# Cross attention in a decoder block: softmax denominators from TensorE, inverse by logarithm on ScalarE, biases added in halves, and an earlier passage from the recurrence

## The reference

```
x = x + slot_attention(layernorm(x))                 # gated recurrence over tokens, 4 heads, 64 slots
q, k, v = layernorm(x) @ Wq.T + bq, ctx @ Wk.T + bk, ctx @ Wv.T + bv      # 16 heads of 8
scores = q k^T * 8**-0.5 + attn_mask; -inf where padded; + fside + fside  # fside: (32, 16, 128, 128), 33.5 MB
x = x + softmax(scores) v @ Wo.T + bo
x = x + experts(layernorm(x))                        # gated low-rank experts around a 128-512-128 network
```

## Time and profile before

| | us |
|---|---|
| three runs | 633.39, 636.18, 636.24 (median 636.18) |
| the profiled execution | 633.74 |
| its span | 632.0 |
| recurrence, roughly | 0 to 225 |
| cross attention, roughly | 225 to 480 |
| experts, roughly | 480 to 632 |

### The profile page before, as it was taken

How to read it: one execution, slowest core, us unless ns; L and a number is a source line. 1 busy time by engine, 2 the same in 40 slices (tenths; PEclk the granted TensorE clock), 3 DMA queues, 4 the chain that set the end, 5 groups by cost and what they waited for, 6 DMA issues and landing times. The chain is left out here.

```text
span 632.0 us, 15993 instructions
## 1 busy us (share of the span) xinstructions
PE 512.1 (81%) x4272; PEld 378.5 (60%) x4272; DVE 499.0 (79%) x2009; ACT 428.9 (68%) x1545; POOL 369.5 (58%) x392
## 2 busy tenths in 40 slices
PE   4788988989987567877777777777766899999986
PEld 3566766766765435555555555555545678888864
DVE  2677777777776359999999999999986588888872
ACT  3667777777774239999999999999984133333321
POOL 6245364364454667888888888888842144444430
PEclk9899999999998869999999999999997599999999
DMA  6900000000000076888888888888700000000000
GB/s 172 229 10 1 1 2 0 0 0 0 2 0 2 9 130 114 153 143 146 147 146 146 144 142 141 141 141 146 133 2 2 0 18 19 17 17 17 19 18 17
DMA packets 84423, 42.37 MB, mean 67 GB/s; under 512 B 4379, under 2 KB 84133, under 8 KB 84389
## 3 DMA queue, kind: packets, MB, share of 16 engines
q1 hardware_dynamic: 83234, 41.63, 35.8%
q10 hardware_dynamic: 1154, 0.33, 0.2%
HBM read 39.86 MB, written 2.10 MB: 66 GB/s over the span
## 5 line engine op out<-in xcount | busy, mean ns | idle before, releaser
L944 ACT ACTIVATE c_P<-c_P,c_min 128x128 f32<-128x128 f32 x512 | 204.7, 461 | 0.0
L1113 POOL TENSOR_TENSOR c_bias<-c_fside,c_cm 128x2048 f32<-128x2048 f32 x32 | 145.5, 4547 | 2.3 <-DVE c_cm L1030 2.3
L944 ACT ACTIVATION_READ_ACCUMULATOR c_P<-c_P,c_min 128x1 f32 x512 | 132.5, 260 | 0.0
L1005 DVE CUSTOM_DVE_ANT_0 c_P<-banks,c_bias 128x128 f32<-128x128 f32 x512 | 117.2, 287 | 8.0 <-issue 3.7
L900 PE MATMUL banks<-ident,c_P 128*128 128x128 f32 x512 | 80.9, 285 | 8.3 <-ACT c_P L944 6.7
L900 PEld LDWEIGHTS banks<-ident,c_P 128*128 128x128 f32 x512 | 57.5, 144 | 23.2 <-ACT c_P L944 13.4
L1040 DVE COPY shared<-banks 128x512 f32<-128x512 f32 x96 | 66.1, 688 | 2.8 <-PE banks L900 2.8
L1455 POOL TENSOR_TENSOR xs<-shared,xs 128x512 fp32r<-128x512 f32 x8 | 10.8, 1345 | 88.5 <-ACT xs L1287 88.5
L1220 PE MATMUL banks<-um,lb_s 128*128 128x512 f32 x192 | 57.7, 417 | 2.7 <-ACT shared L1277 1.9
L748 POOL TENSOR_TENSOR lower<-meanvar,minus_one 128x2 f32<-128x2 f32 x16 | 3.4, 211 | 79.9 <-DVE meanvar L639 79.7
L1277 ACT ACTIVATE shared<-banks,bi_col 128x512 f32<-128x512 f32 x32 | 22.0, 688 | 41.2 <-PE banks L1220 41.2
(11 more groups left out here) (197 smaller groups left out, 1375.4 us busy)
## 6 DMA issues: line engine op xcount, KB each, us to landing
c_fside<-in_fside_Bx16xSxS_dram SPq DMA_DIRECT2D x64, 512.0 KB, 7.1
c_ctx<-in_ctx_dram SPq DMA_DIRECT2D x32, 64.0 KB, 5.2
out_dram<-shared SPq DMA_DIRECT2D x8, 256.0 KB, 2.3
X<-in_x_dram SPq DMA_DIRECT2D x3, 512.0 KB, 5.1
kmask_sb<-in_mask_BxS_bf_dram SPq DMA_DIRECT2D x1, 512.0 KB, 7.4
X<-in_x_dram SPq DMA_DIRECT2D x2, 128.0 KB, 3.4
c_P<-in_L_ffn_wi_dram SPq DMA_DIRECT2D x1, 256.0 KB
c_P<-in_L_ffn_lora_B_dram SPq DMA_DIRECT2D x1, 256.0 KB
```

The costliest lines, as they stand in the source:

```text
L944: last = nc.scalar.activation(P[:, par, h, :], P[:, par, h, :], ACT.Exp, bias=mn[:, par, h:h + 1], scale=-1.0, accum_out=rsx[:, par, h:h + 1])
L1005: last = nc.vector.tensor_tensor_reduce(out=P[:, o, h, :], in0=bank(SCORE_BANKS[i])[:, 128 * j:128 * j + 128], in1=fm[:, o, h, :], scale=- ...
L1113: nc.gpsimd.tensor_tensor(fm[:, q, :, :], fs[:, q, :, :], bc(cm[:], XH), ALU.add).then_inc(C["fm"], 1)
```

## The change

- `exps` no longer writes row sums. Instead `mix_values` runs a second set of 16 products (32 instructions) with blocks of ones in the place of the values, so bank 7, columns 128 to 255, holds each head's sum, already turned and spread over its 8 rows. ScalarE takes the logarithm of that block and the exponential of its negative. Reciprocals, spreading, their transpose and copy go.
- ScalarE copies turned tokens and context in one instruction, and takes over the values copy from VectorE. Its order in a step is exponentials 1, inputs, exponentials 2 and 3, logarithm, inverse, keys, queries, exponentials 0 of the next batch, values, turned weights 3.
- TensorE's order is scores, inputs, weights 0, mix, queries and keys, weights 1, values, weights 2 and 3, output projection. The values product is a semaphore step of its own, apart from the output projection.
- VectorE's order is mask, statistics, score 0, weights 0, aggregate, scores 1 and 2, outputs, weights 1, score 3, normalise, add to the stream, weights 2. The mask block has two buffers.
- Biases are added, waited for and loaded in two halves of 8 heads, and in step n for batch n+1, no longer for n+2. GpSimd's order is first half, output bias, second half, roots, keys spread; its steps before 0 have no biases. Those of batch 0 are added in recurrence steps 4 and 5, of batch 1 in 14 and 15.
- The passage: step -3 comes after recurrence step 15 on GpSimd and VectorE; steps -2, -1, 0, 1 on all engines after recurrence steps 16, 17, 18, 19. The scores of the first two batches use banks 0, 1, 5, 4, with waits on TensorE for what the recurrence still holds.

The diff, cut to its core:

```diff
+            pool_step(pool, nc.gpsimd.memset(head_ones[:].rearrange("p (j w) -> p j w", j=XG)[:, :, 0:XD], 1.0))
...
+        def x_masks(dve, k, q):
+            need(dve, C["fm"], 2 * k - 2)
...
+        def x_biases(pool, k, m, q, half):
+            heads = slice(HALF * half, HALF * half + HALF)
+            need(pool, C["cm"], k + 1)
+            need(pool, s_fs[q][half], 16 * (m + 1))
+            need(pool, C["tt"], 4 * k - 6 + 2 * half)
+            nc.gpsimd.tensor_tensor(fm[:, q, heads, :], fs[:, q, heads, :], bc(cm[:, q, :], HALF), ALU.add).then_inc(C["fm"], 1)
...
+            def values():
                 if project:
+                    need(pe, C["q"], n + 3)
...
+                nc.tensor.matmul(bank(0)[:, 128:256], xcT[:, o, 1, :], x_wT[:, 2, :], start=True, stop=True).then_inc(C["vp"], 1)
...
                 need(pe, C["v"], n)
+                need(pe, C["oT"], n - 1)
+                for w in range(2):
+                    for j in range(XG):
+                        for i in range(NI):
+                            block = vp[:, o, VPAD * i + 32 * j:VPAD * i + 32 * j + 32] if w == 0 else head_ones[:, 32 * j:32 * j + 32]
+                            last = nc.tensor.matmul(bank(7)[32 * i:32 * i + 32, 128 * w:128 * w + 128], block,
+                                                    PTs[:, o, i, 128 * j:128 * j + 128], start=(j == 0), stop=(j == XG - 1))
                 last.then_inc(C["pv"], 1)
+            def project_out():
+                need(pe, C["oT"], n)
+                need(pe, C["x2"], n - 1)
+                need(pe, C["v"], n + 2 if scores else min(n + 1, B))
...
-                    last = nc.scalar.activation(P[:, par, h, :], P[:, par, h, :], ACT.Exp, bias=mn[:, par, h:h + 1], scale=-1.0,
-                                                accum_out=rsx[:, par, h:h + 1])
+                    last = nc.scalar.activation(P[:, par, h, :], P[:, par, h, :], ACT.Exp, bias=mn[:, par, h:h + 1], scale=-1.0)
...
-                nc.scalar.copy(xT2[:], bank(0)[:, 0:128])
-                nc.scalar.copy(cT[:, q, :], bank(0)[:, 128:256]).then_inc(C["T"], 1)
+                nc.scalar.copy(xcT[:, q, :, :].rearrange("p w t -> p (w t)"), bank(0)[:, 0:256]).then_inc(C["T"], 1)
...
+            def denominator_logs():
+                need(act, C["pv"], n)
+                need(act, C["rc"], n - 1)
+                nc.scalar.activation(log_den[:], bank(7)[:, 128:256], ACT.Ln).then_inc(C["ln"], 1)
+            def denominators_inverted():
+                need(act, C["ln"], n)
                 need(act, C["oT"], n - 1)
+                nc.scalar.activation(inv_den[:], log_den[:], ACT.Exp, scale=-1.0).then_inc(C["rc"], 1)
...
-                need(dve, C["fm"], n + 2)
+                need(dve, C["fm"], 2 * n + 3 + i // 2)
...
+            if isinstance(n, int) and n < 0:
+                if norm:
+                    roots()
+                if project:
+                    keys_apart()
+                    output_bias()
+                return
+            biases = scores and not (isinstance(n, int) and n < 1)
+            if biases:
+                x_biases(pool, n + 1, m + q, o, 0)
             if project:
                 output_bias()
-                biases()
-                keys_apart()
+            if biases:
+                x_biases(pool, n + 1, m + q, o, 1)
             if norm:
                 roots()
+            if project:
+                keys_apart()
...
-                need(sp, C["fm"], n - 1)
...
-                    rows = slice(64 * half, 64 * half + 64)
-                    sp.dma_start(fs[rows, q, :, :], bias[rows, :, :]).then_inc(s_fs[q], 16)
+                    heads = slice(HALF * half, HALF * half + HALF)
+                    need(sp, C["fm"], 2 * n - 3 + half)
+                    sp.dma_start(fs[:, q, heads, :], bias[:, heads, :]).then_inc(s_fs[q][half], 16)
...
+            for t in range(4, 6):
+                gsa_peeled(gsa, t)
+                x_biases(pool, 0, 0, 0, t - 4)
             gsa_loop(pool, gsa)
+            for t in range(PAIRS - 2, PAIRS):
                 gsa_peeled(gsa, t)
+                x_biases(pool, 1, 0, 1, t - PAIRS + 2)
             pool.wait_ge(G["xn"], PAIRS)
             x_peeled(cross, -3)
+            gsa_peeled(gsa, PAIRS)
...
+            for k in range(4):
+                x_peeled(cross, k - 2)
+                if k < 3:
+                    gsa_peeled(gsa, PAIRS + 1 + k)
             x_loop(pool, cross)
...
+            pe.wait_ge(G["rt"], PAIRS - 1)
+            pe.wait_ge(G["x1"], PAIRS - 1)
+            x_peeled(cross, 0)
+            pe.wait_ge(C["ptD"], 3)
+            pe.wait_ge(C["ptA"], 1)
+            gsa_peeled(gsa, PAIRS + 3)
             pe.wait_ge(G["un"], PAIRS)
+            pe.wait_ge(G["rt"], PAIRS)
             pe.wait_ge(G["x1"], PAIRS)
+            x_peeled(cross, 1)
             x_loop(pe, cross)
```

More of the change, by code:

```diff
@@ L133, in decoder @@
         lb_s = sb("lb_s", [128, 2, F], fp32r)
-        SHARED = 20736
+        SHARED = 18432
         shared = sb("shared", [128, SHARED])
@@ L949, in inputs_turned, with keys, queries @@
                 need(act, C["Tp"], n + 3)
-                need(act, C["yv"], n + 1)
-                nc.scalar.copy(xT2[:], bank(0)[:, 0:128])
-                nc.scalar.copy(cT[:, q, :], bank(0)[:, 128:256]).then_inc(C["T"], 1)
-            def queries_keys():
+                need(act, C["vp"], n + 1)
+                nc.scalar.copy(xcT[:, q, :, :].rearrange("p w t -> p (w t)"), bank(0)[:, 0:256]).then_inc(C["T"], 1)
+            def keys():
+                need(act, C["qkp"], n + 3)
+                need(act, C["kbd"], n + 2)
+                nc.scalar.activation(kx[:], bank(0)[:, 128:256], ACT.Identity, bias=bk_col[:]).then_inc(C["k"], 1)
+            def queries():
                 need(act, C["qkp"], n + 3)
@@ L975, in x_scalar @@
                 inputs_turned()
-            if finish:
-                reciprocals_turned()
             if attend:
                 exps(n, q, 2)
+                exps(n, q, 3)
+            if finish:
+                denominator_logs()
+                denominators_inverted()
             if project:
-                queries_keys()
-            if attend:
-                exps(n, q, 3)
+                keys()
+                queries()
             if scores:
                 exps(n + 1, o, 0)
+                values()
             if attend:
@@ L1070, in x_vector @@
                 weights_turned(0)
+            if norm:
+                aggregates()
             if scores:
                 score(1)
+                score(2)
+            if finish:
+                outputs()
             if attend:
@@ L1075, in x_vector @@
             if scores:
-                score(2)
-            if finish:
-                outputs()
-            if scores:
                 score(3)
-            if attend:
-                weights_turned(2)
-            if scores:
-                values()
+            if norm:
+                normalise()
             if finish:
@@ L1568, in _ @@
             act.wait_ge(s_xw, XW)
[L1569 to L1576 removed]
+            act.wait_ge(G["s"], PAIRS)
+            act.wait_ge(G["silu"], PAIRS)
+            for k in range(4):
+                x_peeled(cross, k - 2)
+                if k < 3:
+                    gsa_peeled(gsa, PAIRS + 1 + k)
             x_loop(act, cross)
@@ L1611, in _ @@
             gsa_peeled(gsa, 3)
+            dve.wait_ge(s_km, 16)
+            for k in range(2):
+                x_masks(dve, k, k)
             dve.wait_ge(s_x[4], 16)
@@ L1616, in _ @@
             gsa_loop(dve, gsa)
-            for t in range(PAIRS - 2, PAIRS + 1):
+            for t in range(PAIRS - 2, PAIRS):
                 gsa_peeled(gsa, t)
```

171 lines of the change are left out of this document (60 added, 111 removed).

## The result

The changed kernel takes 682.35 us (median of 4 runs, 681.54 to 682.77); the kernel before took 634.78 beside it (4 runs, 631.74 to 636.24). The ratio is 1.0754, with an interval of [1.0707, 1.0802]: 7.5% slower, where 609 us had been forecast. The profiled execution has a span of 681.1 us.

What follows compares the result with a forecast made beforehand. The prediction took ScalarE to bound the kernel, at 7.668 us a step. Span 632.0 - 19.4 (loop) - 8 (passage) + 1.1 (end) = 605.7 us; with the allowance for runs, 609 us, range 598 to 621.

Steps and rivals of the forecast that it cites:

- VectorE's term: VectorE's work per cross step: values copy, reciprocal and its spreading go, so 7.19 - 0.62 = 6.57 us.
- The slower one (5%): Rival, chance 0.05: a bare exponential still takes 0.385 us to the next, ScalarE has 8.2 us a step; 644 us.
- The exponential: ScalarE in the cross step: without accumulator reads the next exponential follows after 0.295 us, not 0.385; 1.5 us less a step.
- The bias half: GpSimd in the cross step: each half of the bias addition takes 2.30 us, bounds 2.0 and 2.52.
- Logarithm and inverse: ScalarE in the cross step: logarithm and exponential of 128 columns add 0.40 and 0.21, together 0.61 us.
- ScalarE's sum: ScalarE's work per cross step after the change: 6.73 us instead of 7.67, bounds 6.0 and 8.2.
- The transfers: Bias loads in the loop: 161 GB/s needed, 179 GB/s available while a transfer runs, so cost zero.
- GpSimd's sum: GpSimd's work per cross step: 6.88 us, bounds 6.3 and 7.3, the largest sum and so the bound unless a chain is longer.
- The chain: Dependent work across engines in the cross loop: 6.95 us a step instead of 7.668, gaining 19.4 us over 27 steps.
- Rival 1: Chance 0.27: chains are longer than their parts, or transfers held at 150 GB/s; step 7.3 us, time 618 us.
- The passage: From recurrence to cross attention: batch 2's scores begin at 236.4 instead of 244.42, 8 us gained, bounds 2 and 12.
- The end: End of cross attention: biases behind expert roots +1.2, exponentials -1.1, last mix +1; sum +1.1 us.

Runs made afterwards that it cites:

- `both`: The changed kernel with the mask's second input read from PSUM bank 7 and the normalisation moved from VectorE to ScalarE: 629.5 us, 0.9924 of the kernel before.
- the bias row: `both` with the output bias added by TensorE, as one more row of the output projection, instead of by GpSimd: 636.41 us, 1.0038 of the kernel before.
- `both_late_stats`: `both` with statistics and normalisation of the first expert group after cross step 30 on VectorE and GpSimd: 618.23 us, 0.9762 of the kernel before.
- `both_late_passage`: `both` with the cross steps at the passage one recurrence step later again, on all engines: 628.41 us, 0.993 of the kernel before.
- `mask_psum`: The changed kernel with only the mask's second input read from PSUM bank 7, for batches 2 to 31: 653.3 us, 1.0306 of the kernel before.

## Why the prediction was wrong

**The step that failed** is VectorE's term: "7.19 - 0.62 = 6.57 us". It took the lengths of mask and normalisation over from the old place to a new one without asking what GpSimd does there. At their new places they are 2.41 and 1.09 us, and VectorE is busy 9.17 us in a step, 2.87 of them with waiting inside these two: the engine believed the least loaded became the bound. Without the 2.87 that is 6.30, so the count of its work was good enough. None of the rivals named this. The slower one (5%) had another mechanism, and that one did not occur.

**Terms that held.** The exponential: 0.295 forecast, 0.295 measured. The bias half: 2.30 forecast, 2.32 to 2.34 from its start to the next. Logarithm and inverse: 0.61 forecast, 0.51 measured (407.27 to 407.78, where the keys' copy starts); ScalarE's sum: 6.73 forecast, 6.84 busy in a step of the kernel after. The transfers: GpSimd's halves show no idle time before them, so none waited for its bias from memory. GpSimd's sum of 6.88 us: `both` has 7.32 (398.70 to 406.02), of which the normalisation's extra work is about 0.42, so 6.90.

**The chain**, "6.95 us", was not reached by any version: 7.33 with the lock gone from the loop, 7.42 with the bias row. Rival 1 (27%) had 7.3 us, but no run is the change with the lock taken away and nothing added, so how much of the 0.4 us is the chain and how much the work that `both` adds to GpSimd and ScalarE stays open. Two slips of the working can be named. The second set of products takes 0.98 us (kernel after, 405.81 to 406.79 on TensorE) instead of 0.81: the "0.22" of waiting that was taken off shows in no row. And the parts of the chain through the keys add up to 13.4 us for two steps, not 13.7, so to 6.7 for one; the choice of 6.95 rested as much on the other two sums. Over the 24 steps the loop of `both` gains 24 x 0.353 = 8.5 us, where the forecast had 24 x 0.72 = 17.

**The passage**, "236.4 instead of 244.42", was wrong by 10.5 us, of which the lock is about 1.3 (245.60 in `both`; `both_late_stats`, with the same passage, has 243.83, but at a higher granted clock, 0.85 against 0.60 from the scores of batch 0 to those of batch 1). VectorE's wait of 7.73 us did go (scores of batch 1 at 231.40 against 236.96). But between the scores of batches 1 and 2 there are 15.5 us now where there were 7.5: TensorE has to drain the last piece of the recurrence after a whole attending step, and VectorE waits 5.12 us for it (kernel after; in brackets the idle time before):

```profile
231.40 0.29 DVE L1044 CUSTOM_DVE_ANT_0 c_P<-banks,c_bias 128x128 f32<-128x128 f32 x1 [1.91 <-issue]
239.68 1.19 PE L493 MATMUL banks<-shared,same_head 128*128 128x256 f32 x2 [0.72 <-issue]
243.95 0.43 DVE L718 TENSOR_TENSOR X<-banks,X 128x256 f32<-128x256 f32 x1 [5.12 <-PE banks L499]
244.59 2.09 PE L884 MATMUL banks<-shared,c_q 32*128 32x512 f32 x8 [0.67 <-issue]
246.91 0.29 DVE L1044 CUSTOM_DVE_ANT_0 c_P<-banks,c_bias 128x128 f32<-128x128 f32 x1 [1.62 <-PE banks L884]
```

The piece itself, from its first product to the addition to the stream, takes 4.3 us (239.68 to 243.95), as the forecast had it ("about 4 us"). What the forecast has no term for is the granted clock. From the scores of batch 1 to those of batch 2, in the kernel after and in the kernel before (TensorE's busy time second, its clock third from the end):

```profile
231.40:246.91 15.51, 10.47 (x40) 7.23 (x41) 7.08 (x40) 7.18 (x23) 6.78 (x7) 0.50 0.06 15
```

```profile
236.96:244.42 7.46, 5.76 (x39) 4.24 (x38) 6.78 (x42) 6.96 (x34) 5.09 (x6) 0.92 0.55 108
```

At 0.50, the lower of TensorE's two levels (1.2 GHz), eight score products take 2.09 us where they took 1.14 before, and four transposes 1.06 where they took 0.66. Between these two batches the order weighs more than the clock: `both_late_stats` has a mean clock of 0.67 between the two batches and needs 15.2 us, `both_late_passage`, with the old order, has 0.76 and needs 8.4. How much of the 10.5 us is the clock wasn't separated.

**The end**, "+1.1 us", is counted in the forecast from the scores of batch 29. From there to the end of the span the kernel before takes 180.71 us, the kernel after 183.77, `both` 184.27: +3.1 and +3.6. The step was "stand behind the roots of the first expert group", priced at these roots alone. But behind them stand both halves of batch 31, and the four normalisations run into them.

Together, for `both` and by the forecast's own cuts (scores of batches 2 and 29): +1.2 at batch 2, -7.2 in the 27 steps, +3.6 behind them, so -2.5 us of span, where the forecast had -8, -19.4 and +1.1, so -26.3. For the kernel after it is +2.5, +43.6 and +3.1.

## What to carry to other kernels

When an order changes, write down for each VectorE instruction that reads and writes SBUF alone which long GpSimd instruction runs beside it in the new order, and give its length as anything up to the length of that. In a profile, such a lock shows as the same instruction with two lengths and no idle time before it: look for a length in the trace of before that doesn't fit its shape (0.74 stood in the earlier trace rows and 0.34 in the earlier trace rows, for the same instruction). An instruction that ends just as the other engine's begins costs nothing yet, but stands on the edge. Cures are an operand in PSUM, another engine, or the gap behind the long instruction; clear all the instructions of that kind at once, since freeing one moves the next into its place.

## What the runs showed of the hardware

- VectorE beside GpSimd: an SBUF-only `scalar_tensor_tensor` of 128 columns took 0.29 to 2.41 us, a `tensor_scalar` 0.34 to 2.12 us, four of these 1.12 to 5.17; with one input in PSUM the first stayed at 0.27 to 0.29. `BATCH_NORM_STATS2`, which has one input, stayed at 0.28 (`mask_psum`). GpSimd's halves, which had started first, kept 2.34 to 2.38 us (kernel after).
- The other way round: a GpSimd addition of 128 columns that started 0.01 to 0.02 us after such a `scalar_tensor_tensor` took 0.59 to 0.61 us instead of 0.45 (kernel before).
- The row sum of an exponential costs 0.095 us of ScalarE's time (0.39 against 0.295 from one start to the next): 37.6 us of the version with late statistics, where ScalarE has the logarithm, the inverse, the values' copy and the normalisation to do as well.
